# Transposing the adapter's output by 32x32 turns on VectorE and a round trip through DRAM, in place of transposes on TensorE

## The reference

```
x = x + LayerNorm(x + relu(x @ W1[lang] + b1) @ W2[lang] + b2) * gamma[lang] + beta[lang]     # adapter, width 128
h = gelu(x @ W1 + b1)                                  # 512 -> 2048
x = x + concat(h @ W2 + b2, h @ We[expert] + be)       # 2048 -> 384 shared and 128 expert columns
```

## Time and profile before

| what | value |
| --- | --- |
| time, 3 runs | 1446.64, 1446.96, 1447.46 us, median 1446.96 |
| span of the profiled execution, first to last instruction | 1444.7 us |
| the profiled execution's own time | not given beside the runs; its span is 2.3 us under their median |
| busy: PE, PEld, DVE, ACT, POOL | 1437.8, 1186.4, 959.4, 525.2, 679.3 us |
| instructions: PE, DVE, ACT, POOL | 6444, 1589, 856, 644 |
| granted TensorE clock | 1.000 of full over the whole span |
| DMA | 263.02 MB, mean 182 GB/s |
| chain that ended last, by engine | PE 94%, POOL 3%, DVE 2%, issue 1% |

### The profile page before, as it was taken

How to read it: one execution, slowest core, us unless ns; L and a number is a source line. 1 busy time by engine, 2 the same in 40 slices (tenths; PEclk the granted TensorE clock), 3 DMA queues, 4 the chain that set the end, 5 groups by cost and what they waited for, 6 DMA issues and landing times.

```text
span 1444.7 us, 19133 instructions
## 1 busy us (share of the span) xinstructions
PE 1437.8 (100%) x6444; PEld 1186.4 (82%) x6444; DVE 959.4 (66%) x1589; ACT 525.2 (36%) x856; POOL 679.3 (47%) x644
## 2 busy tenths in 40 slices
PE   9999999999999999999999999999999999999999
PEld 6878888888888888888888888888888888888887
DVE  7999776785576755677556776568655686544434
ACT  5733453322533235232342323333244322432231
POOL 6987456451483513844148441474423844342101
PEclk9999999999999999999999999999999999999999
DMA  7857466554556445564464644646546454354332
GB/s 228 290 174 258 175 247 227 180 189 140 176 213 206 158 160 180 200 208 146 160 214 165 208 165 142 238 155 207 183 130 248 147 186 160 114 215 160 132 110 88
DMA packets 127908, 263.02 MB, mean 182 GB/s; under 512 B 12226, under 2 KB 84674, under 8 KB 119748
## 3 DMA queue, kind: packets, MB, share of 16 engines
q1 hardware_dynamic: 118020, 158.78, 34.5%
q10 hardware_dynamic: 9792, 103.03, 18.4%
HBM read 224.02 MB, written 37.75 MB: 181 GB/s over the span
## 4 chain that ended last, share of the span: by engine, by line
PE 94%; POOL 3%; DVE 2%; issue 1%; ACT 0%; POOLq 0%; DVEq 0%; ACTq 0%
PE down L259 16%; PE down L257 16%; PE down L258 16%; PE up_b L258 5%; PE up_b L259 5%; PE up_b L257 5%; PE up_c L257 4%; PE up_c L259 4%; PE up_c L258 4%; PE up_a L258 4%; PE up_a L257 4%; PE up_a L259 4%; PE aux L521 1%; PE aux L259 1%; PE aux L258 1%
## 5 line engine op out<-in xcount | busy, mean ns | idle before, releaser
L257 PE MATMUL down<-w,g 128*128 128x512 f32 x1024 | 400.9, 391 | 0.0
L259 PE MATMUL down<-w,g 128*128 128x512 f32 x1024 | 399.1, 390 | 0.0
L258 PE MATMUL down<-w,g 128*128 128x512 f32 x1024 | 398.9, 390 | 0.0
L1333 POOL TENSOR_TENSOR w<-w_raw,ones 128x256 fp32r<-128x256 f32 x125 | 92.9, 743 | 546.3 <-DMA w_raw<-m_we 546.2
L912 DVE TENSOR_TENSOR g<-g_raw,g 128x512 fp32r<-128x512 f32 x256 | 235.2, 939 | 86.0 <-ACT g L680 86.0
L259 PEld LDWEIGHTS down<-w,g 128*128 128x128 f32 x1024 | 192.3, 188 | 40.0
L258 PEld LDWEIGHTS down<-w,g 128*128 128x128 f32 x1024 | 192.4, 188 | 39.2
L257 PEld LDWEIGHTS down<-w,g 128*128 128x128 f32 x1024 | 192.4, 188 | 39.2
L672 ACT ACTIVATE g_raw<-up_a,m_b_sb 128x512 f32<-128x512 f32 x64 | 44.2, 690 | 412.7 <-PE up_a L259 388.0
L907 DVE TENSOR_TENSOR g_raw<-up_b,s 128x512 f32<-128x512 f32 x63 | 43.5, 691 | 220.5 <-PE up_b L259 176.9
L680 ACT CAST g<-g_raw 128x512 fp32r<-128x512 f32 x256 | 159.0, 621 | 8.1
(11 more groups left out here) (234 smaller groups left out, 2516.9 us busy)
## 6 DMA issues: line engine op xcount, KB each, us to landing
w<-w_kept ACTq DMA_DIRECT2D x55, 1792.0 KB, 7.7
w<-w_kept SPq DMA_DIRECT2D x56, 768.0 KB, 5.0
w_raw<-m_we SPq DMA_DIRECT2D x128, 128.0 KB, 4.6
out<-resid SPq DMA_DIRECT2D x64, 256.0 KB, 5.0
xTs_raw<-xT SPq DMA_DIRECT2D x56, 256.0 KB, 3.1
xs<-x SPq DMA_DIRECT2D x56, 256.0 KB, 5.9
w_kept<-w SPq DMA_DIRECT2D x8, 1792.0 KB, 8.4
aw_raw<-a_w SPq DMA_DIRECT2D x29, 256.0 KB, 4.8
```

What stands on the lines that cost most here:

```text
L257: eng.matmul(bank, a_hi, b_hi, start=opens, stop=False, skip_group_check=True)
L258: eng.matmul(bank, a_hi, b_lo, start=False, stop=False, skip_group_check=True)
L259: return eng.matmul(bank, a_lo, b_hi, start=False, stop=closes, skip_group_check=True)
L1333: eng.tensor_tensor(hi, values, ones[:, :, :].to_broadcast([P, 2, PART]), ALU.mult).then_inc(pool_eh[b], 1)
```

## The change

For pairs 1 to 7 x1 is transposed without TensorE. A VectorE turn of one token tile transposes each 32x32 block of the 128x512 tile in place of its block (`dve_turn`); the result of tile t is written at every fourth element, so that the four tiles interleave: after them a row of `turned` holds tokens in the order 4p + t, p being the token's place in its tile. Four transfers per batch put the blocks at their rows in a DRAM tensor, `x1_turned`, in runs of 512 bytes (`keep_turned`), and the four data blocks are loaded from there, two transfers each, into `b12` or into the LO slots of `bo` (`load_blocks`). Casts, differences and subtractions read them in SBUF. Since g now has its columns in the order 4p + t for pairs 1 to 7, the down product's weights are every fourth column of `g` (`tile_columns`), and the output rows stay where they were. The 224 transposes and the waits that stood with them go, as do the two copies of B12 by ACT in each of these pairs.

The turns stand in steps 4 (batch 0, tiles 0 and 1), 5 (batch 0, tiles 2 and 3; batch 1, tiles 0 and 1) and 6 (batch 1, tiles 2 and 3); `turned` shares its place with `xTs` and serves both batches, so the first turn of batch 1 waits for the stores of batch 0. SP stores batch 0 in step 5 and batch 1 in step 6, loads B12 behind that, B11 in step 7 once p1 of that step is done, and B22 and B21 behind p3 and p2. `sp_early` moves from step 5 to the end of step 7. In the first pair the storing of `w1` of its last step moves to the end of the step, the loads of `w2` of step 5 move ahead, the turns of batch 0's second half stand behind the adapter's additions in step 5, and those of batch 1 in step 6.

```diff
+    Q, B32 = 4, 32
+    turned = sb("turned", [P, KC * Q, B32, TT], f32, "xTs")
+    x1_turned = nc.dram_tensor("x1_turned", [PAIRS, 2, KC, P, TOK], f32, kind="Internal").ap()
...
+    def block_raw(of, c):
+
+        return b12[:, c, :] if of == B12 else bo_raw[:, of, c, LO, :]
+
+    TURNED = {B11: (0, 0), B21: (0, 2), B12: (1, 0), B22: (1, 2)}
+
+    def block_landed(eng, m, of, c):
+        b, k = TURNED[of]
+        eng.wait_ge(in_turned[b][k + c], m.front(16, 16))
...
+    def tile_columns(pr, b, k, h, part, t):
+
+        columns = g[:, b, k % 2, h, part, :]
+        if pr is first:
+            return columns[:, t * P:(t + 1) * P]
+        return columns.rearrange("p (n t) -> p t n", t=TT)[:, t, :]
...
-                s = slice(t * P, (t + 1) * P)
-                last = three_passes(eng, down[t][:, :], g[:, b, k % 2, h, HI, s], g[:, b, k % 2, h, LO, s],
+                last = three_passes(eng, down[t][:, :], tile_columns(pr, b, k, h, HI, t), tile_columns(pr, b, k, h, LO, t),
...
         pe_p5(eng, i, m, k)
-        if k == 0:
-            eng.wait_ge(dve_c21, seven(i, 0))
-            pe_transpose(eng, i, 0, 2, up_b)
-            eng.wait_ge(b_low, i.count(6, 4))
-            eng.wait_ge(dve_t, i.count(8, 6))
-            pe_transpose(eng, i, 0, 3)
-        if m and k == GROUPS - 1:
-            eng.wait_ge(dve_x1, m.count(2 * TT, 2 * TT))
-            eng.wait_ge(dve_c21, seven(i, k))
-            pe_transpose(eng, m, 1, 0, up_b)
-            eng.wait_ge(act_h0, m.count(2, 2))
-            pe_transpose(eng, m, 0, 0)
...
             pe_adapter_down(eng, m, b, t + 1, up_c)
-        if m and k == GROUPS - 1:
-            eng.wait_ge(b_low, m.count(6, 1))
-            eng.wait_ge(dve_t, m.count(8, 1))
-            pe_transpose(eng, m, 0, 1)
-            eng.wait_ge(act_gelu, i.count(4 * GROUPS, 4 * k + C11 + 1))
-            pe_transpose(eng, m, 1, 1, up_a)
-            eng.wait_ge(dve_c12, seven(i, k + 1))
-            pe_transpose(eng, m, 1, 2, up_c)
...
         pe_p4(eng, i, k)
-        if m and k == GROUPS - 1:
-            eng.wait_ge(b_low, m.count(6, 2))
-            eng.wait_ge(dve_t, m.count(8, 2))
-            pe_transpose(eng, m, 1, 3)
...
-                act_b12_copy(eng, m, 0, up_b)
-                act_b11_hi(eng, m, 0)
+                act_block_hi(eng, m, B11, 0)
+                act_block_hi(eng, m, B11, 1)
...
+        if m and k == GROUPS - 1:
+            if i is first:
+                act_t_hi(eng, m, T1, 1)
+            act_block_hi(eng, m, B22, 0)
+            act_block_hi(eng, m, B22, 1)
...
+    def dve_turn(eng, m, b, t):
+
+        n = b * TT + t + 1
+        eng.wait_ge(dve_x1, m.count(2 * TT, n))
+        if b == 0 and t == 0:
+            eng.wait_ge(pe_a1, m.count(2 * KC, 2 * KC))
+        if b == 1 and t == 0:
+            eng.wait_ge(kept_turned[0], m.front(16 * Q, 16 * Q))
+        eng.transpose(turned[:, :, :, t], x1[:, b, t, :].rearrange("p (j r) -> p j r", r=B32)).then_inc(dve_turned, 1)
...
+    def dve_t1(eng, m, c):
+        block_landed(eng, m, B12, c)
+        block_landed(eng, m, B11, c)
         eng.wait_ge(pool_tlo, m.count(8, 0))
-        eng.tensor_tensor(t1[:, c, :], b12[:, c, :], bank[:, :], ALU.subtract).then_inc(dve_t, 1)
+        eng.tensor_tensor(t1[:, c, :], b12[:, c, :], block_raw(B11, c), ALU.subtract).then_inc(dve_t, 1)
...
+        if k == 6:
+            dve_turns(eng, m, 1, 0)
...
+        if k == 6:
+            dve_turns(eng, m, 1, 2)
...
+        if k == 5:
+            dve_turns(eng, m, 0, 2)
...
+            if k == 4:
+                dve_turns(eng, m, 0, 0)
             return
+        for c in range(2):
+            dve_t1(eng, m, c)
+            dve_b_lo(eng, m, B11, c)
...
+        if m and k == 5:
+            dve_turns(eng, m, 0, 2)
+        if m and k == GROUPS - 1:
+            dve_t1(eng, m, 0)
+            dve_b_lo(eng, m, B11, 0)
...
+        if m and k in (5, 6):
+            dve_turns(eng, m, 1, 2 * (k - 5))
...
+            if k == 5:
+                dve_sum_c21(eng, i, k)
             dve_moments(eng, m, b, t + 1)
+        if m and k == 4:
+            dve_turns(eng, m, 0, 0)
         if m and k == GROUPS - 1:
+            dve_t1(eng, m, 1)
             dve_b_lo(eng, m, B11, 1)
-            dve_t1(eng, m, 1)
-            dve_t3_t2(eng, m, 0, up_c)
-            dve_b_lo(eng, m, B22, 0, up_c)
         if k == GROUPS - 1:
             dve_g_lo(eng, i, k, C12)
             dve_g_lo(eng, i, k, C22)
+        if m and k == GROUPS - 1:
+            dve_t3_t2(eng, m, 0)
+            dve_b_lo(eng, m, B22, 0)
+            dve_sum_c21(eng, i, k)
+            dve_t3_t2(eng, m, 1)
+            dve_b_lo(eng, m, B22, 1)
 
 
 
...
 
+    def keep_turned(eng, m, b):
+
+        eng.wait_ge(dve_turned, m.front(2 * TT, (b + 1) * TT))
+        blocks = x1_turned[m.index, b, :, :, :].rearrange("c (j i) (q e) -> q i (c j) e", j=Q, q=Q)
+        for q in range(Q):
+            source = turned[q * B32:(q + 1) * B32, :, :, :].rearrange("p j r t -> p j (r t)")
+            eng.dma_start(blocks[q], source).then_inc(kept_turned[b], 16)
+
+    def load_blocks(eng, m, of):
+
+        b, k = TURNED[of]
+        eng.wait_ge(kept_turned[b], m.front(16 * Q, 16 * Q))
+        if of == B12:
+            eng.wait_ge(dve_t, m.count(8, 0))
+        else:
+            eng.wait_ge(pe_p[{B11: 1, B21: 2, B22: 3}[of]], seven(m, 0))
+        for c in range(2):
+            eng.dma_start(block_raw(of, c), x1_turned[m.index, b, k + c, :, :]).then_inc(in_turned[b][k + c], 16)
...
+            if m and k == GROUPS - 1:
+                load_blocks(eng, m, B11)
+            if m and k == 5 and i is not first:
+                keep_turned(eng, m, 0)
...
+                    if k == 5:
+                        first_w2(eng, k, experts)
+                        keep_turned(eng, m, 0)
                     if k == 1:
                         load_xT_pair(eng, m, 0, 2)
-                    keep_w1(eng, k)
+                    if k < GROUPS - 1:
+                        keep_w1(eng, k)
...
-            if after and k == 5:
-                sp_early(eng, after, next_language)
...
-                if k % 2 == 1 and k > 3:
+                if k == GROUPS - 1:
...
+            if m and k == 6 and i is not first:
+                keep_turned(eng, m, 1)
+                load_blocks(eng, m, B12)
...
+            if i is first and k == 6:
+                keep_turned(eng, m, 1)
+                load_blocks(eng, m, B12)
+            if m and k == GROUPS - 1:
+                load_blocks(eng, m, B22)
+                load_blocks(eng, m, B21)
+            if i is first and k == GROUPS - 1:
+                keep_w1(eng, k)
+            if after and k == GROUPS - 1:
+                sp_early(eng, after, next_language)
```

More of the change, by code:

```diff
@@ L139, in build @@
     out_done = [sems(f"out_done{b}_", TT) for b in range(2)]
+    dve_turned, kept_turned = sem("dve_turned"), sems("kept_turned", 2)
+    in_turned = [sems(f"in_turned{b}_", KC) for b in range(2)]
     pe_p = [None, *sems("pe_p", 8)[1:]]
@@ L816, in act_step @@
             return
-        if k == 0 and i is not pairs[1]:
-            act_b22_hi(eng, i, 1)
         if k > 0:
@@ L865, in act_step @@
         act_g(eng, i, k, C22)
-        if i is first and k == GROUPS - 1:
-            act_t_hi(eng, m, T1, 1)
-            act_t_hi(eng, m, T3, 0)
-            act_t_hi(eng, m, T2, 0)
-            act_b22_hi(eng, m, 1)
         if i is first and k in (3, 5):
             act_w2_hi(eng, k)
-        if m and k == GROUPS - 1 and i is not first:
+        if m and k == GROUPS - 1:
[3 more added lines that the diff above has]
+            act_block_hi(eng, m, B22, 1)
             act_t_hi(eng, m, T3, 0)
@@ L1135, in dve_first_step @@
             dve_w2_lo(eng, k - 1)
-        if k == GROUPS - 1:
-            dve_b_lo(eng, m, B11, 0)
-            dve_t1(eng, m, 0)
         if k % 2 == 0:
@@ L1160, in dve_first_step @@
             dve_sum_c21(eng, i, k)
-            if k % 2 == 1:
+            if k % 2 == 1 and k < 5:
                 dve_w2_lo(eng, k)
@@ L1185, in dve_step @@
         if k > 0:
-            dve_sum_c21(eng, i, k - 1)
+            if not (m and k == 6):
+                dve_sum_c21(eng, i, k - 1)
             dve_g_lo(eng, i, k - 1, C21)
         else:
-            if before(i) is not first:
-                dve_sum_c21(eng, before(i), GROUPS - 1)
-                dve_t3_t2(eng, i, 1)
-                dve_b_lo(eng, i, B22, 1)
             dve_g_lo(eng, before(i), GROUPS - 1, C21)
@@ L1195, in dve_step @@
         if k == 0:
-            dve_t4(eng, i, 0, up_b)
-            dve_b_lo(eng, i, B21, 0, up_b)
+            dve_t4(eng, i, 0)
+            dve_b_lo(eng, i, B21, 0)
             dve_t4(eng, i, 1)
@@ L1454, in pool_step @@
             if k == GROUPS - 1:
-                for of, c in t_order(m)[:4]:
+                for of, c in t_order(m)[:2]:
                     pool_t_lo(eng, m, of, c)
@@ L1460, in pool_step @@
             pool_expert(eng, i, 1, k)
```

(5 more changed lines are left out.)

109 lines of the change are left out of this document (49 added, 60 removed).

## The result

The changed kernel takes **1522.01 us** (median, 1521.04 to 1522.4) beside 1447.21 for the kernel before on the same chip: ratio 1.0514, 95% interval 1.0499 to 1.0529. Forecast were 1425.2 us in a range to 1444; it is 75 us slower, on the wrong side of no change.

The account below looks back on a forecast made before the run. PE's own work was taken as the bound: 1444.7 us of span, less 25.7 for transposes, plus 2.4 for step 7 and 1.5 for the first pair, gives 1422.9; the median lies 2.3 above, 1425.2 us, range 1420.5 to 1444.

Parts of the forecast that it names:

- What bounds the kernel; removed from PE, 25.7 us: PE's own work sets the time; dropping 32 transposes (3.67 us) in each of seven pairs saves 25.7 us, none covered.
- Stride-4 weights, 0: Down products of pairs 1 to 7: a load twice as long takes 220 of 227 ns, still fits, costs 0.
- rival 2: Strided weight loads of the down product don't fit: 336 ns per matmul, +293 us, about 1714 us; chance 0.11.
- Rival 3: Strided weight reads disturb PE's streaming operand by a few ns, without a limit; at 9.6 ns 1447 us; chance 0.05.
- The turns, 0.7 us: 56 turns on DVE, 8 in a pair, 0.7 us each (ends 0.69 and 1.38); 0 on the path.
- Low parts and differences, "939 in place of 691 ns", hidden: 14 DVE operations per pair now read SBUF twice: 3.5 us more in steps 7 and 0, hidden by idle time.
- The round trip: Storing and reloading x1 through DRAM: 5.0 us per batch store (ends 3.1 and 8.7), 24 GB/s more traffic, cost 0.
- The tight place, 0.4 us per pair: Step 7: B11 lands after 5.0 us, u2 just in time for p7; 0.4 us per pair, 2.4 in all.
- rival 1: The round trip becomes the wait: late store or B11, p7 waits for u2; 15 us given back, 1438 us; chance 0.17.
- SP's half microsecond: Step 7: SP takes about half a microsecond after p5's start before B11's load goes.
- The end of 8.7: Upper end for B11's landing in step 7, 8.7 us, which would cost 3.3 us per pair.
- The first pair, 1.5 us, ends 0 and 5: DVE is fullest in the first pair; turns ahead of w1's split and later w1 loading cost 1.5 us.

## Why the prediction was wrong

The mechanism of the gain was right, and four terms of the price were not. The sum had 0 for the stride, 0 for the low parts and differences, 2.4 us for B11 and 1.5 for the first pair. The runs showed 22 to 24 us for the stride, 14.9 us of waits for the low part, 32.0 for u2, 4.5 for the first pair's w1, and 22 more at the lower clock behind the waits.

**What bounds the kernel; removed from PE, 25.7 us.** Right. With contiguous weights matmuls follow each other at 226.7 ns and a pair without waits would take the 174.1 us of the sum; the window above comes within 0.9.

**Stride-4 weights, 0.** This step failed, for 24 us, nearly all that the removal gives. It asked only whether a longer load still fits ahead of its matmul. By its own reading it does: 0.21 us beside the 220 ns taken, and rival 2's 336 ns pace did not come. But at stride 2 the load is as good as unchanged and the pace widens all the same, so a cost exists that is not in the fit. Rival 3, "strided reads disturb the streaming operand by a few ns", got 0.05 with the note that no row speaks for it; the runs show its size, 9.0 and 9.7 ns, beside the 9.6 that the text named as the point where all gain is gone, while its mechanism stays open. The Trainium skill, Advanced Engine Details and Errata, section Memory Cachelines, wants two hits on each 16-byte line; the trace agrees that one element per line makes the load longer (295 ns), but two elements per line, which meet the rule, still cost 6.8 ns per matmul. The term had a reasoned bound on the side of a gain and none on the side of a cost.

**The turns, 0.7 us.** They take 1.10 us (1057 to 1136 ns), within the ends of 0.69 and 1.38, and below the prediction's estimate of 1.24 from the Trainium skill's figure (VectorE: DVE Perf Modes, section The three transpose paths). No run tried them alone, and no wait of PE names them.

**Low parts and differences, "939 in place of 691 ns", hidden.** This failed too. The 939 of the earlier trace rows is a mean of two cases, 0.68 us where POOL is idle and up to 1.85 beside it; the trace of before held both. In step 7 and 0 POOL makes the low parts of T3, T2 and T4 at the same time, so the slow case rules just where C21's low part is awaited: 14.9 us of waits. An operand in PSUM had kept these operations out of it. The Trainium skill, SBUF — State Buffer, section SBUF: two separate sides, has this as a rule: a DVE operation with two SBUF inputs and a GpSimd operation that reads SBUF hold their shared ports in turn, and the later one waits for the whole instruction. The trace agrees: DVE's operations start 1.71 and 1.70 us apart and POOL's, between them, 1.77, 1.70 and 1.67, and with an operand in PSUM the same difference took 0.68 us beside POOL. No run here moved POOL's operations away. That the sum per pair (3.5 us) has room in DVE's idle time says nothing on when the results come.

**The round trip.** Step 5, the store, the second batch's turns, w2 and the experts: no wait of PE, as forecast (DVE waits 3.6 us in all for the store). The stores took 2.7 to 5.6 us, median 3.9, where 5.0 was taken. Putting the traffic at "24 GB/s more on 182" and 0 failed: the mean hid a stretch with the engines full, in the kernel before already.

**The tight place, 0.4 us per pair.** The place, the queue behind DVE's wait and the waiting product were right, as rival 1 had them; the landing was mis-sized. 5.0 us were taken, 8.7 was the upper end, 10.5 came. SP's half microsecond was mis-sized too, 2.0 in this pair: it left out the issues of w2 and the experts that stand between the store and B11. Worked with both, the prediction's own chain gives u2 at 927.8 + 2.0 + 10.5 + 4.3 (t1, low part and down sum) = 944.6, where it starts at 944.66. The end of 8.7 was the median of a 768 KB store, `w_kept<-w`. It says nothing of a load that has 2.8 MB issued ahead of it within 2 us; the 1.8 MB of w1 took 7.7 us to land (median) in the kernel before. And the price of a wait was taken as its length: the lower clock behind it adds about 1.5 us to six. Rival 1 held that "only from 3.7 us per pair would nothing remain"; it was 4.3 to 6.4.

**The first pair, 1.5 us, ends 0 and 5.** Mis-sized: 4.73 us at 198.84 for w1 and 4.48 at 211.61 for the low part. The first went to 0.9 once SP loaded w1 ahead of B12, so it was SP's order, named as a risk; the second is the chain of step 0, which was not named for it.

**Left open:** how a strided load slows the matmul beside it; and whether DVE's work at the boundary can be thinned, not only reordered, to come near 1421 us, an estimate: 1447 less the 25.7 of the transposes.

## What to carry to other kernels

Work taken off the bound engine has to be paid by engines and queues at one place in time, not on the average: look at windows of 2 us around the place where the data is needed, at who else's transfers were just issued, and at which other engine works in SBUF at that moment. A strided operand on TensorE is not free because its load is hidden; here it cost nearly as much as the 224 transposes it came with, and moving the same stride to ACT's reads (0.5 us more for a gelu on an engine with room) made it free. A wait of some microseconds cost this PE-bound kernel a quarter to a half more than it lasted, through the clock: 1.5 us on 6.3 in one place, 22 on 48 in the whole.

## What the hardware showed that was not expected

- Weight loads of every second fp32 column take 193 ns, close to contiguous ones (188), and yet the matmuls follow each other at 233 instead of 226.7 ns; at every fourth column the load takes 295 and the pace is 235.
- A 128x512 VectorE operation on two SBUF tiles takes 0.68 us alone and 1.78 us beside a GpSimd one, which is itself 1.7 to 1.8 us then; with one operand in PSUM it took 0.68 us beside GpSimd too.
- A gelu of 128x512 read with a step of four elements takes 1.20 to 1.25 us from SBUF instead of 0.72, and 0.69 from PSUM, as without the step.
- While PE waited 6.3 us the granted clock went to 0.50 within the wait, and it was back 3 us after PE resumed.
- With the 16 DMA engines full at about 360 GB/s, a 256 KB load took 10.5 us from issue to use; without the 1.8 MB load ahead of it 5.8.
